# The stage that joins the first layer: more load sets, tanh two tiles ahead, the gate a tile later, and GpSimd's work on VectorE

## The reference

```
y_sp = y * sigmoid(10 * (y - max(v_th, 0.1)))
s    = (y_sp * silu(z)) @ W_out - xn
g    = silu(bf16(fp8(xn / s_in) @ fp8(kernel / s_k) * (s_in * s_k)) + bias)
x1   = x + s * g
```

## Time and profile before

| | |
|---|---|
| median of 3 runs | 4495.71 us (4488.63 to 4503.1) |
| profiled execution | 4489.22 us, its span 4487.6 us |
| TensorE busy | 3613.8 us, 81% |
| VectorE busy | 3349.0 us, 75% |
| ScalarE busy | 2330.5 us, 52% |
| GpSimd busy | 1420.4 us, 32% |
| ssm_output: first DMA issue, end of the last sum | 1120.1 us, 1342.0 us |

### The profile page before, as it was taken

One profiled execution on the slowest core, in us unless ns is written; L12 is line 12 of the kernel. 1 busy time (PEld: TensorE's weight loads), 2 busy tenths in 40 slices (PEclk: granted clock), 3 DMA queues, 4 the chain that ended last, 5 costly groups with the idle time before them and its releaser, 6 DMA issues. The chain is left out here.

```text
span 4487.6 us, 70677 instructions
## 1 busy us (share of the span) xinstructions
PE 3613.8 (81%) x19727; PEld 2112.8 (47%) x19728; DVE 3349.0 (75%) x4215; ACT 2330.5 (52%) x4148; POOL 1420.4 (32%) x905
## 2 busy tenths in 40 slices
PE   8968888888447967878689999999999996549960
PEld 3445555554334557767633333333333333449960
DVE  8959888888764446655588888888888874658868
ACT  6755555554773432220037777777777773123323
POOL 4458888888232333220100000000000002645530
PEclk9989999999778988989869999999999996569985
DMA  6754444443657842228412232323232303422249
GB/s 216 251 187 163 156 156 155 155 155 118 220 195 164 198 118 83 65 75 227 140 34 69 49 69 49 69 49 69 49 69 49 68 9 93 126 60 90 91 130 303
DMA packets 534113, 537.43 MB, mean 120 GB/s; under 512 B 84720, under 2 KB 439792, under 8 KB 533664
## 3 DMA queue, kind: packets, MB, share of 16 engines
q1 hardware_dynamic: 507328, 475.20, 36.6%
q0 software_dynamic: 13952, 37.74, 2.5%
q10 hardware_dynamic: 12544, 20.98, 1.8%
HBM read 317.41 MB, written 215.19 MB: 119 GB/s over the span
## 5 line engine op out<-in xcount | busy, mean ns | idle before, releaser
L2085 DVE TENSOR_REDUCE at_top<-at_psM 128x1 f32<-128x1024 f32 x1024 | 1205.9, 1219 | 209.0 <-PE at_psM L1934 208.0
L2044 ACT ACTIVATE at_probs<-at_psS 128x512 f32<-128x512 f32 x2048 | 1068.7, 604 | 336.6 <-PE at_psS L1960 326.0
L1960 PE MATMUL at_psS<-at_q,at_k 64*128 64x512 f32 x2048 | 805.3, 470 | 17.9 <-ACT at_probs L2044 8.2
L568 POOL TENSOR_TENSOR sc_prod<-sc_state,sc_c_row 128x1024 f32<-128x1024 f32 x256 | 707.1, 2779 | 156.5 <-DVE sc_state L717 145.5
L1934 PE MATMUL at_psM<-at_k,at_q 62*128 62x512 f32 x2048 | 680.8, 446 | 50.6 <-DMA at_vraw<-scratch_vf 21.8
L717 DVE TENSOR_TENSOR_SCAN sc_state<-sc_dec,sc_psI 128x1024 f32<-128x1024 f32 x256 | 579.1, 2280 | 79.9 <-PE sc_psI L638 48.5
L1934 PEld LDWEIGHTS at_psM<-at_k,at_q 62*128 62x128 f32 x2048 | 322.0, 192 | 600.6 <-DVE at_top L2085 533.6
L1973 PE MATMUL at_psV<-at_probs,at_v 128*32 128x512 f32 x4096 | 552.9, 612 | 34.2 <-ACT at_sums L2049 32.1
L649 PE MATMUL sc_psY<-sc_prod,sc_ident 128*128 128x512 f32 x1024 | 478.9, 608 | 41.2 <-DVE sc_y L703 35.8
L599 ACT ACTIVATE sc_dec<-sc_dt,sc_a_exp 128x1024 f32<-128x1024 f32 x256 | 293.6, 1148 | 328.3 <-DVE sc_state L717 325.2
L1960 PEld LDWEIGHTS at_psS<-at_q,at_k 64*128 64x128 f32 x2048 | 340.3, 185 | 222.3 <-ACT at_probs L2044 214.6
(11 more groups left out here) (395 smaller groups left out, 5127.9 us busy)
## 6 DMA issues: line engine op xcount, KB each, us to landing
sc_c_row<-scratch_bc SPq DMA_DIRECT2D x128, 512.0 KB
scratch_xs<-at_zeros SPq DMA_DIRECT2D x140, 264.0 KB, 4.7
sc_b_row<-scratch_bc SPq DMA_DIRECT2D x64, 512.0 KB, 5.2
ec_y<-scratch_ys SPq DMA_DIRECT2D x32, 512.0 KB, 6.6
ex_x<-scratch_xs SPq DMA_DIRECT2D x39, 264.0 KB, 3.0
si_x<-in_x SPq DMA_DIRECT2D x16, 512.0 KB, 4.4
scratch_xn<-si_xn SPq DMA_DIRECT2D x16, 512.0 KB, 5.0
scratch_x_t<-si_xT SPq DMA_DIRECT2D x16, 512.0 KB, 5.6
```

The lines of the kernel that those rows point to most:

```text
L568: pool.tensor_tensor(prod[:, (n * H + h) % 8, :], state[slot][:], c_row[n % ROWS][:], ALU.mult).then_inc(prod_ready, 1)
L1960: pe.matmul(psS[v % 3][:], rows_of(k4[j], h, 0, GROUP)[:, c * P:(c + 1) * P], rows_of(q4[j], h, 0, GROUP)[:, half * TILE:(half + 1) * TILE ...
L2044: act.activation(probs[:, slot(j, v), :], psS[v % 3][:], ACT.Exp).then_inc(act_done, 1)
L2085: dve.tensor_reduce(top[j % 2][:, h, c:c + 1], psM[t % 2][:], AX.X, ALU.max, negate=True).then_inc(maxed, 1)
```

## The change

- y, z and xq get four sets. SyncE loads the first four tiles at the start (x and xn of tiles 0 and 1 stand between those of tiles 1 and 2). Its step(i) is now: wait for x1(i-1), store it, load x and xn of tile i+1, wait for a(i) and psG(i), load y, z and xq of tile i+4. x and xn keep two sets.
- spike and open_ get two buffers. ScalarE's step(i) is: gs, glog, grec of tile i, tanh of tile i+2 (spikes), the copies g0 of tile i+1 (product). gden goes to VectorE as a tensor_scalar in bf16. The copies take their scales from per_tok directly, and the tok buffers and copies go.
- VectorE's step(i) is: g1(i); g(i-1); gden(i); sg(i-1) and x1(i-1); ysp, zsp, a of tile i+1; s(i). g1 and grec get two buffers, g keeps one. GpSimd has no program in the stage any more.
- TensorE's order of work and its waits stay, with four sets to read from.
- The loops go over four tiles a turn: the first four and the last four tiles are written out.

The diff, without the old buffers, the old programs of ScalarE and VectorE, and TensorE's:

```diff
+        two, SETS = range(2), 4
+        y, z, xq = ([m.sb(f"{n}{k}", [P, H, TILE], t) for k in range(SETS)] for n, t in (("y", F32), ("z", F32), ("xq", BF16)))
+        x, xn = ([m.sb(f"{n}{k}", [P, SUB, D]) for k in two] for n in ("x", "xn"))
+        spike, open_, a = ([m.sb(f"{n}{k}", [P, H, TILE]) for k in two] for n in ("spike", "open", "a"))
+        ysp, zsp = m.sb("ysp", [P, H, TILE]), m.sb("zsp", [P, H, TILE])
+        g1, grec = ([m.sb(f"{n}{k}", [P, SUB, D], BF16) for k in two] for n in ("g1_", "grec"))
+        g0, gs, gden, g = (m.sb(n, [P, SUB, D], BF16) for n in ("g0", "gs", "gden", "g"))
+        glog, sg = m.sb("glog", [P, SUB, D]), m.sb("sg", [P, SUB, D])
+        s, x1 = ([m.sb(f"{n}{k}", [P, SUB, D]) for k in two] for n in ("s", "x1"))
+        psO, psG = ([m.ps(f"{n}{k}", [P, SUB, D]) for k in two] for n in ("psO", "psG"))
...
+        def turns(eng, step):
+
+            for i in range(SETS):
+                step(i, i)
+            with eng.Fori(1, NT // SETS - 1) as turn:
+                for k in range(SETS):
+                    step(turn * SETS + k, k)
+            for i in range(NT - SETS, NT):
+                step(i, i % SETS)
+
+        def known(i):
+            return isinstance(i, int)
+
+        def yz_at(i, k):
+            return (i - k) * (48 // SETS) + 48
...
-                def step(i, par, loads):
-                    if loads:
-                        sp.wait_ge(o_psum, i + 1)
-                        m.settle(sp)
-                        load_yz(i + 2, par)
+                def store(i, par):
                     sp.wait_ge(x1_ready, i + 1)
...
-                    sp.dma_start(rows("x1", i), x1[par][:]).then_inc(x1_st, 16)
-                    if loads:
-                        load_x(i + 2, par)
-
-                with sp.Fori(0, NT // 2 - 1) as turn:
-                    for par in range(2):
-                        step(turn * 2 + par, par, True)
-                for par in range(2):
-                    step(NT - 2 + par, par, False)
-                sp.wait_ge(x1_st, 16 * NT)
-
-            @block.gpsimd
-            def _(pool):
-                for i, par in pairs(pool, NT):
-                    pool.wait_ge(s_ready, i + 1)
-                    pool.wait_ge(g_ready, i + 1)
-                    pool.wait_ge(x1_ready, i)
-                    pool.tensor_tensor(sg[:], s[par][:], g[par][:], ALU.mult).then_inc(sg_ready, 1)
-                    pool.wait_ge(sg_ready, i + 1)
-                    pool.wait_ge(x1_st, 16 * i)
-                    pool.tensor_tensor(x1[par][:], sg[:], x[par][:], ALU.add).then_inc(x1_ready, 1)
+                    sp.dma_start(rows("x1", i), x1[par][:]).then_inc(x1_st[par], 16)
+
+                def step(i, k):
+                    if not known(i) or i:
+                        store(i - 1, (k + 1) % 2)
+                        if not known(i) or i + 1 < NT:
+                            load_x(i + 1, (k + 1) % 2)
+                    if not known(i) or i + SETS < NT:
+                        sp.wait_ge(a_ready, i + 1)
+                        sp.wait_ge(g_psum, i + 1)
+                        m.settle(sp)
+                        load_yz(i + SETS, k)
+
+                load_yz(0, 0)
+                load_yz(1, 1)
+                load_x(0, 0)
+                load_x(1, 1)
+                load_yz(2, 2)
+                load_yz(3, 3)
+                turns(sp, step)
+                store(NT - 1, (NT - 1) % 2)
+                for k in two:
+                    sp.wait_ge(x1_st[k], 16 * NT // 2)
...
+                def spikes(i, k):
+                    act.wait_ge(yz_loaded[k], yz_at(i, k))
+                    if not known(i) or i >= 2:
+                        act.wait_ge(ysp_ready, i - 1)
+                        act.wait_ge(zsp_ready, i - 1)
                     for h in range(H):
-                        act.activation(spike[:, h, :], y[par][:, h, :], ACT.Tanh, bias=vbias[:, h:h + 1],
+                        act.activation(spike[k % 2][:, h, :], y[k][:, h, :], ACT.Tanh, bias=vbias[:, h:h + 1],
                                        scale=5.0).then_inc(spike_ready, 1)
-                    act.wait_ge(zsp_ready, i)
-                    act.activation(open_[:], z[par][:], ACT.Tanh, scale=0.5).then_inc(open_ready, 1)
-
-                def product(i, par):
+                    act.activation(open_[k % 2][:], z[k][:], ACT.Tanh, scale=0.5).then_inc(open_ready, 1)
+
+                def product(i, k):
                     act.wait_ge(g_psum, i + 1)
-                    act.wait_ge(tok_ready, i + 1)
-                    act.wait_ge(g1_ready, i)
-                    for k in range(SUB):
-                        act.activation(g0[:, k, :], psG[par][:, k, :], ACT.Copy, scale=tok[par][:, k:k + 1]).then_inc(g0_ready, 1)
-
-                def step(i, par, more):
-                    if more:
-                        front(i + 1, 1 - par)
-
+                    if not known(i) or i:
+                        act.wait_ge(g1_ready, i)
+                    for c in range(SUB):
+                        act.activation(g0[:, c, :], psG[k % 2][:, c, :], ACT.Copy,
+                                       scale=per_tok[:, bass.ds(i * SUB + c, 1)]).then_inc(g0_ready, 1)
+
+                def step(i, k):
                     act.wait_ge(g1_ready, i + 1)
-                    act.activation(gs[:], g1[:], ACT.Exp, scale=-1.0).then_inc(gs_ready, 1)
-                    act.wait_ge(gs_ready, i + 1)
-                    act.activation(gden[:], gs[:], ACT.Identity, bias=1.0).then_inc(gden_ready, 1)
+                    if not known(i) or i:
+                        act.wait_ge(gden_ready, i)
+                    act.activation(gs[:], g1[k % 2][:], ACT.Exp, scale=-1.0).then_inc(gs_ready, 1)
                     act.wait_ge(gden_ready, i + 1)
                     act.activation(glog[:], gden[:], ACT.Ln).then_inc(glog_ready, 1)
                     act.wait_ge(glog_ready, i + 1)
-                    act.wait_ge(g_ready, i)
-                    act.activation(grec[:], glog[:], ACT.Exp, scale=-1.0).then_inc(grec_ready, 1)
-                    if more:
-                        product(i + 1, 1 - par)
-
-                front(0, 0)
+                    if not known(i) or i >= 2:
+                        act.wait_ge(g_ready, i - 1)
+                    act.activation(grec[k % 2][:], glog[:], ACT.Exp, scale=-1.0).then_inc(grec_ready, 1)
+                    if not known(i) or i + 2 < NT:
+                        spikes(i + 2, (k + 2) % SETS)
+                    if not known(i) or i + 1 < NT:
+                        product(i + 1, (k + 1) % SETS)
+
+                spikes(0, 0)
+                spikes(1, 1)
+                act.wait_ge(tok_ready, 1)
                 product(0, 0)
-                one_ahead(act, step)
+                turns(act, step)
...
+                dve.tensor_scalar(per_tok[:], bad[:], both[:, 0:1], None, ALU.add).then_inc(tok_ready, 1)
+
+                def front(i, k):
+                    par = k % 2
+                    dve.wait_ge(yz_loaded[k], yz_at(i, k))
                     dve.wait_ge(spike_ready, H * i + H)
-                    dve.wait_ge(a_ready, i)
-                    dve.scalar_tensor_tensor(ysp[:], spike[:], 1.0, y[par][:], ALU.add, ALU.mult).then_inc(ysp_ready, 1)
+                    if not known(i) or i:
+                        dve.wait_ge(a_ready, i)
+                    dve.scalar_tensor_tensor(ysp[:], spike[par][:], 1.0, y[k][:], ALU.add, ALU.mult).then_inc(ysp_ready, 1)
                     dve.wait_ge(open_ready, i + 1)
-                    dve.scalar_tensor_tensor(zsp[:], open_[:], 1.0, z[par][:], ALU.add, ALU.mult).then_inc(zsp_ready, 1)
+                    dve.scalar_tensor_tensor(zsp[:], open_[par][:], 1.0, z[k][:], ALU.add, ALU.mult).then_inc(zsp_ready, 1)
                     dve.wait_ge(zsp_ready, i + 1)
                     dve.wait_ge(ysp_ready, i + 1)
-                    dve.wait_ge(o_psum, i)
+                    if not known(i) or i >= 2:
+                        dve.wait_ge(o_psum, i - 1)
                     dve.scalar_tensor_tensor(a[par][:], ysp[:], 0.25, zsp[:], ALU.mult, ALU.mult).then_inc(a_ready, 1)
 
-                def step(i, par, more):
+                def opened(i, par):
+                    dve.wait_ge(grec_ready, i + 1)
+                    if not known(i) or i:
+                        dve.wait_ge(sg_ready, i)
+                    dve.tensor_tensor(g[:], g1[par][:], grec[par][:], ALU.mult).then_inc(g_ready, 1)
+
+                def joined(i, par):
+                    dve.wait_ge(g_ready, i + 1)
+                    dve.wait_ge(s_ready, i + 1)
+                    if not known(i) or i:
+                        dve.wait_ge(x1_ready, i)
+                    dve.tensor_tensor(sg[:], s[par][:], g[:], ALU.mult).then_inc(sg_ready, 1)
+                    dve.wait_ge(sg_ready, i + 1)
+                    if not known(i):
+                        dve.wait_ge(x1_st[par], (i - par) * 8)
```

(59 more changed lines are left out.)

31 lines of the change are left out of this document (10 added, 21 removed).

## The result

The changed kernel takes 4449.03 us (median of 4 runs, 4448.79 to 4451.37), the one before 4498.91 (4 runs, 4488.63 to 4503.1). The ratio is 0.9893 with a 95% interval of 0.9877 to 0.9908: faster, by a little over 1%. The profiled executions took 4489.22 and 4448.79 us, 40.4 us apart; the forecast was 33.7.

What follows compares the result with a forecast made beforehand. A ring of two tiles through two load sets was taken as the bound. 15 steps at 10.7 us less 1.3 make 159.2 against 190.0; with the tail 33.7 us less, so 4462 from the median, range about 4449 to 4479.

Steps and rivals of the forecast that it cites:

- The ring of two tiles through the loads: From tanh through gate, GpSimd sums, store and loads to tanh two tiles on: 25.43 us, said to bound the stage.
- The new period: From one gs to the next in the changed stage: the walked operations and handoffs sum to 10.66, say 10.7 us.
- a rival at 0.10: Before Ln on ScalarE: the table load hides the wait for gden, 15 times 0.47 us less, 4455; chance 0.10.
- The step without a tanh near the end: Step 14 of the stage: without tanh, VectorE's 7.1 us set the step, making it 1.3 us shorter.
- GpSimd and VectorE: VectorE's g1: with GpSimd idle it takes 0.68 us on all tiles, where it took 2.04 beside GpSimd.
- VectorE behind ScalarE: After gden, VectorE needs 7.1 us against ScalarE's 8.4, so it waits 1.3 us for g0 and is the next bound.
- the floor of 8.2 us: Transfers of the stage: 2.88 MB a tile at 353 GB/s take 8.2 us, below every engine's sum, so hidden.
- slow transfers: Stage transfers: if loads and stores give only 228 GB/s, the period stays 12.6 us, 4493; chance 0.07.
- late rows: Loads of x and xn, still in two sets, land late: at 23 us landing, a 14.5 us period, 4520; chance 0.04.
- the long g1: VectorE's exposed g1 stays long even without GpSimd: 1.36 us more on 15 tiles, 20.4 us, 4482; chance 0.03.
- Start, tail: Stage ends: first gs at 1139.5 where it was 1139.62; last gs to last sum 9.5 us, 2.9 less.
- the dearer handoffs: Exposed waits between ScalarE and VectorE: gden 0.69 and 0.1 us more in three waits, period 11.3, 4471; chance 0.14.

Runs made afterwards that it cites:

- four sets alone: Kernel before with four sets of y, z and xq instead of two and nothing else: median 4456.48 us, ratio 0.9911 to the kernel before.
- the sums on VectorE alone: Kernel before, still two sets, with only sg and x1 moved from GpSimd to VectorE right behind g: 4439.12 us, ratio 0.9958 to before.
- the gate by tanh: Changed kernel with tanh of tile i+2 behind the copies and one tanh replacing gs, Ln, grec, gden and both table loads: 4401.67 us, ratio 0.9872 to before.
- the later round: Changed kernel run again, unaltered, beside other kernels and the kernel before: median 4419.61 us, ratio 0.9902 to the kernel before.

## Why the prediction was right, and where it was off

**The bound.** Right. The ring of two tiles through the loads set the period. Two experiments shorten it in two places (four sets alone, the sums on VectorE alone), and both land within 0.2 us a tile of what the earlier trace rows give; in the new order with two sets the same arithmetic gave 19.3 us, and the 13 steps that wait for a load took 19.3.

**The new period.** I walked 10.66 us from gs to gs. Eleven of the 14 terms hold, these among them: g1 0.69 with its handoffs, the copies and tanh, and gden is as long as I had it (0.43). What failed is that "handoff 0.03, gden 0.43, handoff 0.04" stand in the sum at all. The load does not wait for gden; it runs from the end of gs and is longer (1.28) than the whole round trip. I had this as a rival at 0.10, with 0.47 us a tile as its price. The price was right (15 times 0.47 are 7.1 of the 7.4 us), the chance too low. The reason I gave against it was the earlier trace rows, a load that stood idle behind TensorE. Its line has two waits in the code, one for the product and one for the store of the gate before it, and Ln has only one here. The experiment with a second wait turned the one case into the other. So the chain of the sum is right, but one wait in it does not exist, because I read a row without the count of waits at its line.

The step without a tanh near the end is 0.83 us shorter than the others and not 1.3. It is the same error again: VectorE sets that step, 9.34 us where the forecast has 9.4, and the other steps are the shorter ones.

```profile
1268.36 1.06 ACT L855 ACTIVATE so_gs<-so_g 128x1024 bf16<-128x1024 bf16 x1 [0.76 <-DVE so_g L967]
...
1278.54 1.06 ACT L855 ACTIVATE so_gs<-so_g 128x1024 bf16<-128x1024 bf16 x1 [0.76 <-DVE so_g L967]
...
1287.88 1.06 ACT L855 ACTIVATE so_gs<-so_g 128x1024 bf16<-128x1024 bf16 x1 [2.09 <-DVE so_g L967]
```

**GpSimd and VectorE.** Right: g1 took 0.69 us on all tiles. The earlier trace rows showed it stretched beside GpSimd and short without. The experiment with the sums on GpSimd shows that the stretch goes with whatever runs beside GpSimd's operation (gden, ysp), not with g1. The Trainium skill's lock (SBUF — State Buffer, "Practical consequences") covers an instruction with two SBUF inputs, such as g1 and ysp. For a tensor_scalar, such as gden, it holds only in a two-port mode, and no trace shows the mode. The times agree with it: gden ends at 1215.73, 0.29 us behind GpSimd's sg, and ysp at 1219.02, 1.07 us behind GpSimd's x1. It is VectorE that is held up most: GpSimd's two operations took 2.13 and 2.35 us there and 2.12 and 2.60 in the kernel before, where x1 took 2.34 on the last tile.

**VectorE behind ScalarE.** Right: 0.86 us of wait for g0 where I had 1.3; with the period 0.47 us shorter that is the same number. Its busy time was 127.7 us where I had about 133, so that forecast was some 5 us too high; ScalarE's 138.2 stands against 137.

**The transfers.** Right for this kernel: no engine waits for a load, at 83% and 269 GB/s. But the floor of 8.2 us was about half a microsecond too low, as the gate by tanh shows. The sum used it only to call the transfers hidden, and they were. The rivals of slow transfers and late rows are out; so is the long g1.

**Start, tail.** Right within 0.5 us: the start 0.1 us earlier, the tail 9.0 us for 9.5, which is the wait for gden once more.

**The median.** Forecast 4462, measured 4449, at the very edge of a range that began at about 4449. 7.4 us of the 13 are the stage, the table load above all, less 0.6 that the rest of the program took back. The other 6 are the starting point. I subtracted from a median that lay 6.5 us above the profiled execution, while the median of the changed kernel lies 0.2 above its own. Why the runs of the kernel before spread over 14.5 us and those of the changed kernel over 2.6 (7.7 in the later round) is open. Redone, the range is 4448 (4455 less half of the runs' spread) to 4478, and the period of the dearer handoffs is 11.2 us and not 11.3.

**What each part gave** (stage, us): four sets alone 33.3 of 41.1. The other parts together give the remaining 7.8, and taking either of two of them back costs more than that: with the sums on GpSimd the new order loses 13.5, with gden on ScalarE 16.1. The gate a tile later and the missing tok copies were not tried by themselves. On the other hand, the place of tanh in front of the copies costs 12.5, which an exchange of two calls gives back.

## What to carry to other kernels

When an engine waits for a load on every tile, follow the load back to what frees its buffer before asking how fast it is: here 14.8 us of a ring of 25.4 were work of the engines and not the load, and more buffers took the whole ring off the path. When an operation is handed to another engine, put it where the first engine has something to do that needs neither result, such as a table load or the next tile's work: the round trip for gden was free beside the table load, and the one for g1 cost 0.76 us a tile behind the copies and nothing under the tanh. And count the waits at a line before reading what its first instruction waited for.

## What the runs showed of the hardware

A table load in front of an activation with one wait did not wait: it started 0.01 us after the last ScalarE operation while gden was still to run. With two waits it stood idle for 0.54 us until gden had ended. One more wait, which holds nothing up by itself, thus cost 7.5 us in the stage. Which of two waits holds the load is not settled: gden's stands second at its line, and in the earlier trace rows, whose line has two waits as well, the load stood idle for the product, which stands first.

A 16-bit tensor_scalar of 128x1024 on VectorE took 0.427 us alone and 1.97 us when it came 0.45 us behind a GpSimd tensor_tensor; scalar_tensor_tensor of the same size in f32 took 1.22 and 3.38 us.

With five loads and one store a tile the DMA engines gave 228 GB/s at 69% busy, 269 at 83% and 320 at 97%, which makes an estimated 324 to 330 at full, where the loads of the start gave 353 at a share of 1.02.
